# Attention rounds of four head pairs: scores and transposes side by side in TensorE's order

## What is computed

```python
x = x + attn_a(layernorm(x), ...)   # sigmoid Q,K,V; A = +-0.9*exp(-|tQ-tK|/0.5)+0.9; A @ V @ Wo + bo
x = x + ffn(layernorm(x), ...)      # silu(x@wg) * (x@wu) @ wd, hidden 384, weights int * 1/127
x = x + attn_b(layernorm(x), ...)   # 16 heads of 64, causal softmax over 256 rows, out projection
x = x + ffn(layernorm(x), ...)
```

## Time and profile before

| | |
|---|---|
| median of the runs | 319.6 us (319.6 to 320.65, three runs) |
| the profiled execution's own time | 320.58 us |
| its span, first to last instruction | 318.7 us |
| PE busy, share of the span | 307.9 us, 97% |
| DVE / ACT / POOL busy | 278.4 / 249.7 / 228.6 us |
| granted TensorE clock | 1.00 in all windows |

### The profile page before, as it was taken

How to read it: one execution, slowest core, us unless ns; L and a number is a source line. 1 busy time by engine, 2 the same in 40 slices (tenths; PEclk the granted TensorE clock), 3 DMA queues, 4 the chain that set the end, 5 groups by cost and what they waited for, 6 DMA issues and landing times.

```text
span 318.7 us, 10095 instructions
## 1 busy us (share of the span) xinstructions
PE 307.9 (97%) x3186; PEld 268.4 (84%) x3186; DVE 278.4 (87%) x1117; ACT 249.7 (78%) x848; POOL 228.6 (72%) x305
## 2 busy tenths in 40 slices
...
DMA packets 6419, 5.83 MB, mean 18 GB/s; under 512 B 864, under 2 KB 5856, under 8 KB 6368
## 3 DMA queue, kind: packets, MB, share of 16 engines
...
q10 hardware_dynamic: 288, 0.20, 0.2%
...
## 4 chain that ended last, share of the span: by engine, by line
PE 92%; POOL 2%; DVE 2%; ACT 2%; issue 1%; POOLq 0%; ACTq 0%
PE bank L606 14%; PE bank L583 9%; PE bank L399 9%; PE bank L571 8%; PE bank L400 8%; PE bank L401 7%; PE bank L568 6%; PE bank L459 4%; PE bank L460 3%; PE bank L469 3%; PE bank L417 3%; PE bank L448 2%; PE bank L527 2%; PE bank L526 2%; PE bank L528 2%; PE bank L430 1%
## 5 line engine op out<-in xcount | busy, mean ns | idle before, releaser
L1019 POOL TENSOR_TENSOR prob<-prob,row_inv 128x256 f32<-128x256 f32 (+1 forms) x128 | 102.9, 832 | 34.8 <-DVE row_inv L921 34.8
L719 ACT ACTIVATE prob<-neg_s,neg_max 128x256 f32<-128x256 f32 x128 | 64.2, 501 | 0.0
L717 ACT ACTIVATE prob<-neg_s,neg_max 128x128 f32<-128x128 f32 x128 | 50.8, 397 | 9.7 <-DVE neg_max L897 9.2
L897 DVE CUSTOM_DVE_ANT_0 neg_s<-bank,mask 128x256 f32<-128x256 f32 x128 | 53.8, 420 | 0.0
L606 PE MATMUL bank<-early,v 128*64 128x256 f32 (+1 forms) x512 | 46.7, 330 | 0.0
L931 DVE TENSOR_TENSOR qk<-bank,bqk 128x512 f32<-128x512 f32 x64 | 42.9, 685 | 2.0 <-PE bank L401 1.5
L606 PEld LDWEIGHTS bank<-early,v 128*64 128x64 f32 x512 | 31.9, 137 | 13.4 <-issue 3.0
L895 DVE CUSTOM_DVE_ANT_0 neg_s<-bank,mask 128x128 f32<-128x128 f32 x128 | 36.6, 286 | 4.3 <-PE bank L571 3.6
L571 PE MATMUL bank<-qk 64*128 64x256 f32 x256 | 38.4, 377 | 0.0
L399 PE MATMUL bank<-rt_hi,wqkv_hi 128*128 128x256 f32 x128 | 38.1, 298 | 0.0
L906 DVE COPY early<-bank 128x384 f32<-128x384 f32 x64 | 33.8, 551 | 3.5 <-PE bank L583 3.4
...
## 6 DMA issues: line engine op xcount, KB each, us to landing
...
```

The source lines that it names most:

```text
L717: nc.scalar.activation(prob[:, r, e, 0:P], neg_s[:, m % SCORE_BUFS, e, 0:P], ACT.Exp, bias=neg_max[:, q, 2 * e:2 * e + 1], scale=-1.0, acc ...
L719: nc.scalar.activation(prob[:, r, e, P:SC], neg_s[:, m % SCORE_BUFS, e, P:SC], ACT.Exp, bias=neg_max[:, q, 2 * e + 1:2 * e + 2], scale=-1. ...
L897: nc.vector.tensor_tensor_reduce(out=neg_s[:, m % SCORE_BUFS, e, P:SC], in0=S[:, P:SC], in1=mask[:], scale=-SCORE_SCALE, scalar=3e38, op0= ...
L1019: nc.gpsimd.tensor_tensor(pr, pr, inv, ALU.mult).then_inc(p_norm, 1)
```

## The change

Only `ORDER` and `BANKS` change. All jobs are the same, 459 on PE in both lists; the number of `hot` jobs is 19 in both. In the new PE list four pairs make a round: four `scores` and, next to them, the four `transposes` of the round before, then two `sum` in a row. Some F jobs still stand inside. ACT's, DVE's and POOL's lists and the banks are new throughout. The lines that matter here (the list of PE: start, three rounds, end; then the start of DVE's and POOL's lists):

```diff
     "PE": """
-        hot.0 hot.1 hot.2 hot.3 hot.4 hot.5 hot.6 lntA.0 hot.7 hot.8 qkv0.0 qkv1.0 qkv2.0 mean.0 hot.9 hot.10 hot.11 lntA.1
-        vwo.0 aout.0 hot.12 qkv2.1 qkv0.1 qkv1.1 lntF.0 mean.1 hot.13 gF0.0 gF1.0 gF2.0 bo.0 lntA.2 dbF.0 qkv2.2 qkv1.2 vwo.1
-        hot.14 qkv0.2 vwo.2 lntB.0 aout.1 qk.0 qk.1 qk.2 scores.0 scores.1 scores.2 lntF.1 qk.3 v3.0 gF0.1 qk.4 gF1.1 qk.5 qk.6
...
-        scores.31 qkv2.6 lntB.4 sum.27 transposes.28 qk.32 qk.33 v2.4 transposes.29 scores.32 scores.33 transposes.30 v0.4
-        lntF.5 qkv1.6 qk.34 qk.35 gF2.5 v1.4 gF1.5 scores.34 scores.35 qk.36 qk.37 vwo.6 gF0.5 lntP.2 sum.29 transposes.31
...
-        transposes.61 sum.59 transposes.62 transposes.63 sum.61 sum.63 lntP.6 pre1.0 pre0.0 out1.7 out0.7 gP0.6 gP1.6 dnP.5
-        gP2.6 hot.15 lntP.7 hot.16 hot.17 gP0.7 gP1.7 gP2.7 hot.18 dbP.5 dnP.6 dbP.6 dbP.7
+        hot.0 hot.1 hot.2 hot.3 hot.4 hot.5 hot.6 hot.7 hot.8 hot.9 lntA.0 hot.10 qkv1.0 qkv0.0 qkv2.0 hot.11 mean.0 lntA.1
+        vwo.0 qkv1.1 qkv0.1 qkv2.1 aout.0 mean.1 bo.0 vwo.1 hot.12 hot.13 lntA.2 lntF.0 hot.14 aout.1 gF0.0 gF1.0 qkv0.2 gF2.0
+        qkv2.2 qkv1.2 hot.15 lntA.3 dbF.0 hot.16 vwo.2 mean.2 hot.17 lntA.4 qkv1.3 qkv0.3 hot.18 qkv2.3 lntB.0 qkv2.4 mean.3
+        lntF.1 v1.0 v3.0 qk.0 qk.1 qk.2 qk.3 v2.0 scores.0 scores.1 scores.2 scores.3 aout.2 lntA.5 gF2.1 qkv0.4 gF1.1 vwo.3
...
+        qkv0.7 qk.32 qk.33 qk.34 qk.35 v2.4 scores.32 scores.33 v0.4 scores.34 transposes.28 transposes.29 scores.35
+        transposes.30 transposes.31 sum.29 sum.31 lntP.2 qk.36 qk.37 qk.38 gP0.2 gP2.2 qk.39 v1.4 scores.36 scores.37 dnF.5
+        scores.38 scores.39 transposes.32 transposes.33 transposes.34 transposes.35 mean.6 gP1.2 dbF.5 otB.3 sum.33 sum.35 otr.3
...
+        qk.63 otB.6 scores.62 transposes.57 scores.63 otr.6 v1.7 v3.7 dnP.5 transposes.58 transposes.59 transposes.60 sum.57
+        sum.59 transposes.61 lntP.6 transposes.62 transposes.63 sum.61 sum.63 pre1.0 gP1.6 pre0.0 out0.7 out1.7 gP2.6 dbP.5
+        gP0.6 lntP.7 gP0.7 gP1.7 gP2.7 dnP.6 dbP.6 dbP.7
...
     "DVE": """
-        lnsA.0 xnA.0 ga.0 lntA.0 gb.0 lnsA.1 wf.0 mean.0 sign.0 w0.0 lntA.1 bv.0 aout.0 lnsF.0 lnsA.2 xnF.0 w4.0 lntF.0 mean.1
-        gF0.0 gF1.0 gF2.0 bo.0 sign.1 lntA.2 dbF.0 lnsB.0 w2.0 xnB.0 lnsA.3 lntB.0 aout.1 lnsF.1 qk.0 qk.1 qk.2 mask.0 mask.1
+        lnsA.0 ga.0 xnA.0 lnsA.1 lntA.0 gb.0 wf.0 mean.0 lntA.1 sign.0 w4.0 bv.0 lnsA.2 aout.0 mean.1 lnsF.0 bo.0 sign.1 xnF.0
+        w0.0 lntA.2 lntF.0 lnsA.3 aout.1 gF0.0 gF1.0 gF2.0 lnsA.4 lnsF.1 dbF.0 lntA.3 lnsB.0 mean.2 xnB.0 lntA.4 lnsA.5 lntB.0
...
     "POOL": """
-        lnsA.0 ga.0 lnsA.1 sv.0 xb.0 stdp.0 lnsF.0 w5.0 lnsA.2 w3.0 stdp.1 xb.1 sv.1 sv.2 lnsB.0 w1.0 lnsA.3 lnsF.1 ol.0 xb.2
+        lnsA.0 ga.0 xb.0 xb.1 lnsA.1 sv.0 stdp.0 sv.1 lnsA.2 lnsF.0 stdp.1 lnsA.3 w5.0 sv.2 lnsA.4 lnsB.0 lnsF.1 lnsA.5 stdp.2
...
 BANKS = {
...
-    "t0": "3566670462126601705753105353603241647554456255320434144111417162",
-    "t1": "0741241131354567076111234764335002754376722334563101363440765647",
+    "t0": "6362635377217164237702746523545465650602341663746412107032520316",
+    "t1": "2735124150543073546624163165036007307267615225635235523520316570",
```

More of the change, by code:

```diff
@@ L56 @@
[L56 to L63, removed]
@@ new lines @@
+        transposes.2 transposes.3 dbF.1 sum.1 sum.3 lntA.6 qkv0.5 mean.4 lntF.2 qkv1.5 otA.0 mean.5 lntB.1 qkv2.5 qkv2.6 gF1.2
+        gF0.2 v3.1 gF2.2 qk.8 qkv1.6 qk.9 qk.10 v0.1 qk.11 scores.8 scores.9 scores.10 v2.1 transposes.4 transposes.5
+        transposes.6 scores.11 transposes.7 sum.5 sum.7 dnF.2 qk.12 qk.13 qk.14 qk.15 dbF.2 scores.12 scores.13 otB.0 v1.1 otr.0
+        transposes.8 scores.14 scores.15 transposes.9 transposes.10 transposes.11 sum.9 sum.11 lntB.2 aout.4 vwo.5 qk.16 lntP.0
@@ new lines @@
+        qk.17 qk.18 v2.2 gP2.0 qk.19 lntF.3 v0.2 vwo.6 scores.16 scores.17 scores.18 v1.2 transposes.12 transposes.13 scores.19
+        transposes.14 transposes.15 sum.13 sum.15 lntF.4 gF2.3 gF1.3 gP0.0 gP1.0 gF0.3 otA.1 otB.1 qk.20 qk.21 qk.22 qk.23 v3.2
+        otr.1 dnF.3 scores.20 scores.21 dbF.3 dnP.0 aout.5 transposes.16 transposes.17 transposes.18 scores.22 scores.23
+        transposes.19 sum.17 sum.19 lntB.3 gF1.4 gF2.4 gF0.4 v0.3 lntP.1 qk.24 qk.25 qk.26 gP2.1 qk.27 gP1.1 v1.3 v2.3 scores.24
@@ new lines @@
+        scores.38 scores.39 transposes.32 transposes.33 transposes.34 transposes.35 mean.6 gP1.2 dbF.5 otB.3 sum.33 sum.35 otr.3
+        v3.4 qkv1.7 lntB.5 aout.6 dnP.2 qk.40 otA.4 lntP.3 dbP.2 v0.5 qk.41 lntF.6 gP0.3 v1.5 gF1.6 scores.40 gF2.6 qk.42 qk.43
+        qkv2.7 scores.41 gF0.6 v2.5 scores.42 scores.43 transposes.36 transposes.37 gP1.3 transposes.38 transposes.39 sum.37
+        sum.39 gP2.3 mean.7 dnF.6 qk.44 dbF.6 otB.4 qk.45 otr.4 qk.46 qk.47 scores.44 transposes.40 transposes.41 vwo.7 v3.5
@@ L89 @@
[L89 to L96, removed]
```

201 lines of the change are left out of this document (106 added, 95 removed).

## The result

The changed kernel takes 325.91 us (median; 325.15 to 326.89) against 319.61 before: a ratio of 1.019 with an interval of 1.015 to 1.023, or +6.3 us. The forecast was 319.6 with a range up to 322.7. The granted clock differs between executions: in the four of the changed kernel its mean is 0.99, 0.995, 1.00 and 1.00 (326.89, 326.43, 325.39 and 325.15 us), in the profiled one of before 1.00. So at full clock the changed kernel still takes 325.2 to 325.4 us, some 5.7 more than before.

A forecast was written before the change was run, and what follows sets the result against it. PE, busy 243.93 of 244.00 us from 56 to 300 us, was taken as the bound. The terms -2.9 + 0.9 + 0.2 + 1.0 + 0.8 = 0.0 left the forecast at 319.6 us, range 317.4 to 322.7.

The forecast's parts named there:

- PE: mode changes and neighbours: PE's list: 15 fewer mode changes at 0.17 us and 10 fewer scores behind transposes at 0.05, put at 2.9 us less.
- lntP.6 and dnP.5 ahead of sum.63: End of the middle: these jobs move from where PE waits to where each job counts, put at 0.9 us more.
- gP1.6 ahead of out: Behind sum.63: gP1.6 now stands ahead of out, 0.5 us against 0.3 for lntP.6 gone there, put at +0.2 us.
- waits in the middle: Rounds in the middle: new PE waits for banks, 0.4 us at transposes.34 plus weaker places, put at +0.8, from 0.4 to 3.
- PE's sum comes through whole: Faster rival: the start loses nothing and waits stay at 0.4 or hide in each other; 317.7 us, chance 0.22.
- I found three or four weaker places of this kind: Middle: bank waits at scores.17, scores.35 and transposes.61 among them, estimated at 0.1 to 0.2 us each.
- the bursts starve: Slower rival: DVE's copies lag four transposes in a row, 0.2 us waiting in each of 16 rounds; 322.8 us, chance 0.22.
- chain of four steps: Start: lntA.0 (with aout.0), lntF.0, lntB.0 and qk.0 each come later, qk.0 by 6.1 us, against 5.0 of work done earlier.
- some 0.1 to 0.3 comes back: Between 32 and 56 us: of 1.1 us lost at the start, 0.1 to 0.3 returns as the former list's waits shrink.
- I cost that at nothing: End: the four hot jobs are gone, the waits they filled are under 2 us each; put at no cost.
- The price in parentheses: End: if the clock fell for the last three gP jobs, their 1.4 us would double.
- PE waits under 1.5 us in the sum of the middle: Sign that the forecast is right: PE's waits in the middle total under 1.5 us, the longest at transposes.34.

## Why the prediction was wrong, by its steps

| us | put | measured |
|---|---|---|
| PE: mode changes and neighbours | -2.9 | -2.4 |
| lntP.6 and dnP.5 ahead of sum.63 | +0.9 | +0.8 |
| gP1.6 ahead of out | +0.2 | +0.3 |
| start, at equal clock | +1.0 | +2.4 |
| waits in the middle | +0.8 | +4.15 |
| clock | 0 | +1.1 in the profiled execution |
| sum | 0.0 | +6.35 |

**PE's list.** Right in kind and nearly in size. There is a slip in the addition: 2.6 and 0.5 make 3.1, not 2.9, so that the terms give -0.2 and a forecast of 319.4; nothing in what follows hangs on it. The price of a change was put at 0.17 and measures 0.168; that of alternating scores and transposes at 0.05, and measures 0.05. The list without waits is 2.4 shorter instead of 2.9. Where the missing 0.5 or more lies isn't shown; neighbours among F jobs, which I had taken to be free, are a candidate, but I didn't break the list down. The rival "PE's sum comes through whole" fails at the other terms.

**The waits of the middle** are the term that decided, put at 0.8 with an upper end of 3. The step that failed is "I found three or four weaker places of this kind". The method, to look for bursts and reused banks, found the largest place (transposes.34: 0.4 put, 0.47 measured). But the weaker ones that it named came to next to nothing (scores.35 0.03, scores.17 and transposes.61 under 0.025), while there are 37 places, 0.13 us each in the mean, and most aren't bursts. My reading is that an order laid anew meets inputs and banks that aren't ready in many places; the run with exchanged neighbours has 21 such places, but there the other lists had changed as well, and the 14 exchanges with room around them made none. The rival "the bursts starve" was right about the reader's pace (1.9 us go with short copies, none in before) and by chance about the size (3.2 put, 4.15 measured); it was wrong that `sum` is where it shows, and its sign, a DVE busy with 95%, never came: DVE is busy with 220.10 of 243.30 us in the middle, 90%, against 92% in the earlier trace rows. The Trainium skill's remark (TensorEngine Tiling (Array Packing), PSUM Bottleneck) that tiled work may leave the readout of PSUM as the bound agrees in kind with those 1.9 us, though TensorE stays the bound here (242.18 of 243.30 us busy in the middle); using both engines for it, which the page advises there, this kernel does already.

**The start.** The chain of four steps was right, each a little too short: qk.0 comes 6.98 later instead of 6.1, against 5.04 of work done (5.0 put). The failed step is "some 0.1 to 0.3 comes back": between qk.0 and sum.3 another 0.5 is lost. Of the 2.4, the three extra hots ahead of lntA.0 make 0.7 at most: without them qk.0 came at 37.25 in place of 37.99, since the input isn't there much before, and in that run the first matmuls became fast earlier, too.

**The clock.** "I cost that at nothing" failed. The row that I rested on, an idle time of 1.74 us without a fall, was one gap in one execution. What precedes the fall at the end is three windows with 0.39, 0.16 and 0.28 of PE busy, but the same list doesn't always bring a fall: at the start the clock fell in the profile of after and in none of the three runs with short copies, at the end in after and two of those three. The price in parentheses was of the right size: 1.4 put for a fall at the last gP jobs, 1.1 measured in before without its end hots and 0.7 in after. The fall at the start (from 16.2 us, into mean.1 and bo.0) was not considered; it costs 1.4, found from lntA.0 to qk.0: 31.01 us against 29.60 in the run with both copies short, whose granted clock stays at 1.00 there. As lntA.0 itself came about 1.0 earlier than it would have with before's late rise, the clock adds 1.4 + 0.7 - 1.0 = 1.1 in this pair of traces.

The signs that I had named: the prices held, and the longest wait's place. qk.0 near 38 did not: it stands at 39.30 in the profile of after, and the 37.99 above is from an execution whose first matmuls became fast sooner, worth about 1 us, than in the trace of before that the forecast started from; 6.98 later than 32.03 would be 39.0. lntA.0 came at 8.29 and not near 9.3 for the same reason. And "PE waits under 1.5 us in the sum of the middle" didn't.

What stays open: why the rounds of sum.19 to sum.27 run with next to no wait while those ahead and behind don't. The time of the copies explains 1.9 us; the remaining 2.3 us of new waits are listed by who came last, but in the run with other lists much the same sum stood partly in other places, so that no cause of them is shown.
